# Source buckets padded to 256 rows instead of 512, four parts in a unit, adds one unit behind

## The reference

```python
Wh = h @ W + b
row, col = edge_index[0], edge_index[1]          # the edge's source, the edge's destination
sc = softplus(deg_coeff[0] * deg_v + deg_coeff[1])
dot = sum(Wh[row] * Wh[col], -1);  nr, nc = norms of Wh[row], Wh[col]
sim = dot / maximum(nr * nc, EPS)
base = adj_v * sc * (row != col)
prop_pos = segment_sum((base * relu(sim))[:, None] * Wh[col], row)
prop_neg = segment_sum((base * -relu(-sim))[:, None] * Wh[col], row)
out = scale * (coeff[0] * prop_pos + coeff[1] * prop_neg + coeff[2] * Wh)
x = layernorm(x + out)
```

## Time and profile before

| | us |
|---|---|
| median of 3 runs | 9442.85 (9428.52 to 9460.71) |
| the profiled execution | 9496.65 |
| its span, first to last instruction | 9494.9 |
| unit loop in it, first pick to last add | 8290.0 to 9446.6 |

### The profile page before, as it was taken

The page is one execution under the profiler, slowest core; times in us unless marked ns, Lnnn a source line. Parts: engine busy times, 40 slices in busy tenths (PEclk is TensorE's granted clock), DMA queues, the critical chain, the costliest instruction groups (busy, mean ns, idle before and its releaser), DMA issues. The chain is left out here.

```text
span 9494.9 us, 103424 instructions
## 1 busy us (share of the span) xinstructions
PE 5779.2 (61%) x22770; PEld 3507.7 (37%) x22771; DVE 4579.2 (48%) x10542; ACT 3305.8 (35%) x6399; POOL 5102.6 (54%) x5308
## 2 busy tenths in 40 slices
PE   0068788888840777777777524444443444499997
PEld 0034343434320333333333222222222222299997
DVE  2545555555542333333333353444444444477777
ACT  0023333333320333333333311111111111299997
POOL 5666666666656666666666555566655656500000
PEclk9978887878765777777777755555555555599998
DMA  8233333333321333333333211111111111122221
GB/s 325 80 93 111 109 107 110 109 110 106 112 62 49 98 98 103 102 103 103 106 103 104 81 30 55 52 52 53 52 51 51 53 51 53 47 59 59 60 59 52
DMA packets 566846, 800.69 MB, mean 84 GB/s; under 512 B 163210, under 2 KB 307466, under 8 KB 566506
## 3 DMA queue, kind: packets, MB, share of 16 engines
q1 hardware_dynamic: 371944, 482.15, 16.8%
q0 software_dynamic: 172640, 195.75, 9.3%
q10 hardware_dynamic: 22178, 121.99, 3.2%
HBM read 497.93 MB, written 301.41 MB: 84 GB/s over the span
## 5 line engine op out<-in xcount | busy, mean ns | idle before, releaser
L696 POOL DMA_INDIRECT rows_by_src_bucket<-arena,put_idx x1568 | 1532.8, 978 | 1019.2 <-DVE arena L1342 549.3
L625 POOL DMA_INDIRECT G<-h_rows,src_idx x1568 | 1483.2, 946 | 852.7 <-issue 456.2
L625 POOL DMA_INDIRECT G<-in_x,src_idx x1470 | 1395.7, 949 | 808.5 <-issue 432.2
L1172 DVE TENSOR_TENSOR_SCAN xd_t<-same,xd_t,ps_two 128x512 f32<-128x512 bf16 x588 | 749.1, 1274 | 1044.1 <-remote 870.0
L746 PE MATMUL ps_gv<-attr,w_attr 65*128 65x512 f32 x1568 | 1104.1, 842 | 220.4 <-issue 126.3
L749 PE MATMUL ps_gv<-arena,w_src 128*128 128x512 f32 x1568 | 1044.3, 803 | 0.0
L728 PE MATMUL ps_two<-ident,inj 128*128 128x128 f32 x2352 | 445.1, 322 | 938.1 <-DMA inj<-first_edge_rows 648.2
L928 ACT COPY arena<-ps_out 128x512 f32<-128x512 f32 x392 | 230.5, 588 | 2124.7 <-remote 1864.0
L813 PE MATMUL ps_pos<-arena 128*128 128x392 f32 x390 | 316.3, 914 | 1017.1 <-DVE arena L1195 621.9
L1234 DVE TENSOR_SCALAR arena<-ps_gv 128x512 f32<-128x512 f32 x392 | 266.5, 680 | 1228.5 <-remote 607.4
L752 PE MATMUL ps_gv<-xd_t,w_dst 128*128 128x512 f32 x1568 | 773.8, 616 | 3.5 <-issue 3.5
(11 more groups left out here) (226 smaller groups left out, 10251.1 us busy)
## 6 DMA issues: line engine op xcount, KB each, us to landing
inj<-first_edge_rows SPq DMA_DIRECT2D x588, 256.0 KB
running_sums<-arena SPq DMA_DIRECT2D x392, 256.0 KB
same<-same_dst SPq DMA_DIRECT2D x1176, 64.0 KB
rows_by_src_bucket<-zeros ACTq DMA_DIRECT2D x98, 703.5 KB
first_edge_rows<-zeros ACTq DMA_DIRECT2D x56, 896.0 KB
attr<-in_attr_t SPq DMA_DIRECT2D x392, 128.0 KB
G<-h_rows,src_idx POOLq DMA_INDIRECT x1568
rows_by_src_bucket<-arena,put_idx POOLq DMA_INDIRECT x1568
```

The lines of the kernel that those rows point to most:

```text
L625: pool.indirect_dma_start(out_, None, table_in, bass.IndirectOffsetOnAxis(ap=index, axis=0)).then_inc(s, 16)
L696: pool.indirect_dma_start(bucket_d, bass.IndirectOffsetOnAxis(ap=put_idx[:, buf, k:k + 1], axis=0), put[:, buf, k], None).then_inc(s_added ...
L1172: v.tensor_tensor_scan(xd_t[:, buf % 2], same[:, buf], ps_inj, xd_t[:, 1 - buf % 2, COLS - 1:COLS], ALU.mult, ALU.add).then_inc(s_scan, 1)
```

## The change

Buckets are padded to 256 rows (a *part*, `PART`) instead of 512, and a unit of 1024 rows holds four parts instead of two halves. With the same 200,704 edges the padding allows for 98 x 256 rows instead of 98 x 512: `UNITS` goes from 248 to 224, `UTRIPS` from 31 to 28. So each unit has four buckets: PE picks two tiles with each register, and loads eight registers in every second unit; PE's sum accumulates over two tiles, into four ranges of the bank; DVE has four adds of 64 columns instead of two, and loads four registers in every unit. DVE's add follows with a lag of one unit instead of two. The parts' bucket numbers need seven columns instead of four (`IDS`), and the table `bucket_at` lies in the first partition of the tile `attr`, which the convolutions have finished with.

```diff
-UNIT = 2 * COLS
+PARTS = 4
+PART = 2 * P
+UNIT = PARTS * PART
 NU = 8
-UNITS = -(-(EP // COLS + NT) // (2 * NU)) * NU
+UNITS = -(-(EP // PART + NT) // (PARTS * NU)) * NU
+IDS = UNITS * PARTS // P
...
-        bucket_units = bucket_d[0:BROWS].rearrange("(u a p j) f -> u p a (j f)", a=2, p=P, j=TILES)
+        bucket_units = bucket_d[0:BROWS].rearrange("(u q p j) f -> u p q (j f)", q=PARTS, p=P, j=2)
...
-        bucket_at = sb("bucket_at", [1, 2, COLS], I32)
...
+        bucket_at = attr[0:1].rearrange("p b c -> p (b c)")[:, 0:2 * UNITS * PARTS].bitcast(I32).rearrange(
+            "p (k n) -> p k n", k=2)
...
             def pick(h, buf):
-                if buf % NB == 0:
-                    pe.wait_ge(s_halves, 1)
+                if buf % 2 == 0:
+                    pe.wait_ge(s_parts, 1)
                     buckets[:] = nc.values_load_multi_w_load_instructions(
-                        bucket_at[0:1, 0, ds(h * (2 * NU) + 2 * buf, 2 * NB)], engines=(mybir.EngineType.PE,),
+                        bucket_at[0:1, 0, ds(h * (PARTS * NU) + PARTS * buf, 2 * PARTS)], engines=(mybir.EngineType.PE,),
...
             def sum_unit(h, buf):
...
+                for k in range(SLOTS):
+                    mm = pe.matmul(summed[buf % 2][:, k // 2], onehot[:, buf % NB, k], w_msg[:, buf % 2, k],
+                                   start=k % 2 == 0, stop=k % 2 == 1)
                 mm.then_inc(s_outs, 1)
...
-                for c in range(TILES):
-                    then(v.tensor_scalar(junk_, ends, half_id[:, c:c + 1], 0.0, ALU.is_le, ALU.add,
-                                         accum_out=half_bucket[:, c:c + 1]))
+                for c in range(IDS):
+                    then(v.tensor_scalar(junk_, ends, part_id[:, c:c + 1], 0.0, ALU.is_le, ALU.add,
+                                         accum_out=part_bucket[:, c:c + 1]))
...
             def add_unit(h, buf):
-                if buf % 2 == 0:
-                    dve.wait_ge(s_halves, 2)
-                    homes[:] = nc.values_load_multi_w_load_instructions(
-                        bucket_at[0:1, 1, ds(h * (2 * NU) + 2 * buf, 4)], engines=(mybir.EngineType.DVE,), min_val=0,
-                        max_val=(NT - 1) * D,
-                        skip_runtime_bounds_check_because="a count of bucket ends, at most NT - 1")[1]
+                dve.wait_ge(s_parts, 2)
+                homes = nc.values_load_multi_w_load_instructions(
+                    bucket_at[0:1, 1, ds(h * (PARTS * NU) + PARTS * buf, PARTS)], engines=(mybir.EngineType.DVE,),
+                    min_val=0, max_val=(NT - 1) * D,
+                    skip_runtime_bounds_check_because="a count of bucket ends, at most NT - 1")[1]
                 dve.wait_ge(s_outs, udone(h, buf))
-                for a in range(2):
-                    home = H[:, ds(homes[2 * (buf % 2) + a], D)]
-                    add = v.tensor_tensor(home, home, summed[buf % 2][:, a], ALU.add)
-                    if a == 0:
+                for q in range(PARTS):
+                    home = H[:, ds(homes[q], D)]
+                    add = v.tensor_tensor(home, home, summed[buf % 2][:, q], ALU.add)
+                    if q < PARTS - 1:
                         then(add)
                 add.then_inc(s_hadd, 1)
                 dve.wait_ge(s_hadd, udone(h, buf))
 
-            pipeline(dve, (weigh, 0), (add_unit, 2), steps=steps, per=8 * NU, n=NU, trips=UTRIPS)
+            pipeline(dve, (weigh, 0), (add_unit, 1), steps=steps, per=10 * NU, n=NU, trips=UTRIPS)
```

More of the change, by code:

```diff
@@ L242, in gnn @@
         onehot = tile(NB, SLOTS, P)
-        rows = [t.rearrange("p (a c) -> p a c", a=2) for t in (
+        rows = [t.rearrange("p (q c) -> p q c", q=PARTS) for t in (
             *(whole[:].rearrange("p b c -> p (b c)")[:, k * 2 * TILES * RW:(k + 1) * 2 * TILES * RW]
@@ L588, in load_unit @@
                     sp.wait_ge(s_wm, udone(h, buf, NU))
-                load(rows[buf], bucket_units[ds(h * NU + buf, 1)].rearrange("u p a c -> p (u a) c"), s_unit[buf])
+                load(rows[buf], bucket_units[ds(h * NU + buf, 1)].rearrange("u p q c -> p (u q) c"), s_unit[buf])
             pipeline(sp, (load_unit, 0), n=NU, trips=UTRIPS)
@@ L854, in pick @@
                 pe.wait_ge(s_dotted, udone(h, buf, 1))
[L855 to L858 removed]
+                for k in range(SLOTS):
+                    col = k % TILES * (D + 1)
+                    mm = pe.matmul(ps_two[:, k // TILES, col:col + D + 1], onehot_t[:, buf % 2, k],
+                                   wh_flat[:, ds(buckets[PARTS * (buf % 2) + k // 2], D + 1)], start=True, stop=True)
                 mm.then_inc(s_wr, 1)
@@ L863, in sum_unit @@
                 pe.wait_ge(s_hadd, udone(h, buf, 2))
-                for a in range(2):
-                    for j in range(TILES):
-                        mm = pe.matmul(summed[buf % 2][:, a], onehot[:, buf % NB, a * TILES + j],
-                                       w_msg[:, buf % 2, a * TILES + j], start=j == 0, stop=j == TILES - 1)
+                for k in range(SLOTS):
+                    mm = pe.matmul(summed[buf % 2][:, k // 2], onehot[:, buf % NB, k], w_msg[:, buf % 2, k],
+                                   start=k % 2 == 0, stop=k % 2 == 1)
                 mm.then_inc(s_outs, 1)
@@ L1324, in _ @@
             for k, width in enumerate((D + 1, D)):
-                v.tensor_scalar(bucket_at[0:1, k], ps_out[0:1], float(width), None, ALU.mult).then_inc(s_halves, 1)
+                for c, table in enumerate((ps_out, ps_pos)):
+                    n = min(COLS, IDS * P - c * COLS)
+                    turn = v.tensor_scalar(bucket_at[0:1, k, c * COLS:c * COLS + n], table[0:1, 0:n], float(width), None,
+                                           ALU.mult)
+                turn.then_inc(s_parts, 1)
             def place_group(i):
@@ L1359, in weigh @@
             def weigh(h, buf):
-                now = rows[buf].rearrange("p a (j f) -> p a j f", f=RW)
-                flat = rows[buf].rearrange("p a (j f) -> p (a j) f", f=RW)
+                flat = rows[buf].rearrange("p q (j f) -> p (q j) f", f=RW)
+                now = flat.rearrange("p (a j) f -> p a j f", a=2)
                 picked = ps_two[:, :, 0:TILES * (D + 1)].rearrange("p a (j f) -> p a j f", f=D + 1)
```

47 lines of the change are left out of this document (23 added, 24 removed).

## The result

| | before | after |
|---|---|---|
| median, chip A, us | 9449.92 | 9486.42 |
| ratio, 95% interval | | 1.0042 [1.0031, 1.0053] |
| median, chip B, us | 8119.79 | 8161.10 |
| ratio, 95% interval | | 1.0043 [1.0028, 1.0057] |
| profiled execution on A / its span | 9496.65 / 9494.9 | 9506.64 / 9504.9 |

The change makes the kernel slower by 0.42% as the ratio gives it; the two medians are 36.5 us apart. Chip B runs the stages ahead of the unit loop much faster, but its ratio is the same. In the two profiled executions on A those stages differ by 35 us in after's favour (the first pick is at 8255.4 instead of 8290.0), which hides most of the loop's loss in them; on the faster chips of the experiments variants of both kernels have the first pick between 6915 and 6930 us. So I read the change from the loop alone.

A forecast was written before the change was run, and what follows sets the result against it. It took PE, DVE and ACT as all near the unit loop's bound. -12 + 3 - 1 + 70 = +60 gave a span of 9555, taken over to the median as 9503 us; range 9425 to 9600.

The forecast's parts named there:

- DVE sets the pace: Unit loop: two more adds make DVE's cycle 4.97 us, above PE's 4.43; trips 40.5 us against 36.97.
- The term of -12 us: Unit loop: 28 trips of 40.5 us, 1134 us, against 1146; the saved units are nearly eaten by the adds.
- Register loads at nothing: DVE's load of four registers in every unit, 344 ns, is covered by L1382: nothing; uncovered, up to 39 us.
- The rival of 601 ns: DVE's register load takes 601 ns, first add 0.25 us later in each unit: +46, 9489 us before falls; chance 0.05.
- The lag costs nothing: Adds one unit behind: PE's sum is ready before DVE comes to its add, so no new wait costs time.
- ACT and the loads of units free: Unit loop: ACT fits in 4.62 us a unit; unit loads stay hidden, up to 1 us at the loop's start.
- The clock: Unit loop: PE's idle gaps lower its clock at every second trip's end, 14 falls of 5 us: +70 us; forecast's chance 0.63.
- PE's ordinary gap: PE idles 0.53 us ahead of its sum in every unit, between 0.37 that held the clock and 0.66 that fell.
- The clock holds: Rival: no falls in the unit loop, only DVE's pace counts: -10, 9433 us; chance 0.22.
- The adds are covered: Rival: the unit keeps its 4.62 us by PE's or ACT's pace: -111 + 2, 9334 us; chance 0.05.
- The clock stays low: Rival: PE keeps the lower clock for most of the unit loop, 1888 us against 1146: 10180 us; chance 0.05.
- The terms of +3 and -1: Setting up, with more counts, transposes, writes and two adds at the end: +3 us; smaller bucket clearing: -1 us.

The follow-up runs named there:

- One filler at the trip's end: The changed kernel with four more PE transposes in one unit of eight, the turn at the trip's end; ratio to the kernel before 0.9984.
- the kernel with two adds: The changed kernel without the adds of the third and fourth part of each unit; one execution, trips 35.71 us, unit loop 1005.6 us.
- the fillers: Extra PE transposes in the changed kernel: four in one unit of eight, ratio to the kernel before 0.9984; four in every unit, 1.0001.
- two fillers: The changed kernel with two more PE transposes in every unit; one execution, unit loop 1141.3 us.
- the kernel with split adds: The kernel before with each add of 64 columns cut into two of 32, four adds in a unit; one execution, 9666.17 us.

## Why the prediction was right

The forecast was 9503 us by a few falls of the clock; the median is 9486.42. The signs it named are there: a granted clock of 0.92 in the loop, the adds in fours, trips of two lengths. Step by step:

- **DVE sets the pace: right.** I had 4.97 us a unit and 40.5 a trip; after has 40.55. The first rows of two ordinary units stand 4.97 apart (8617.82 and 8622.80). Of the parts, the adds' step of 0.35 is (1.27 - 0.22) / 3, and a trip's end costs what the earlier trace rows gave. The term of -12 us is -10.4.
- **Register loads at nothing: right by an accident of the layout.** 344 ns at the median, as in the earlier trace rows. The rival of 601 ns did not come. But that the duration belongs to four registers at such addresses, and not to the instruction, I could not know, and did not ask.
- **The lag costs nothing: right,** and it spares some 10 us against a lag of two, which I had put at nothing once DVE is the bound. In the kernel before, where PE waits for adds, it gives 20 us even with the longer load.
- **ACT and the loads of units free: right.** DVE does not wait for the root in after, nor for a unit.
- **The clock: right in kind and place, too dear.** I had 14 falls at 5 us, 70 us; it was 14 at 4.12, 57.7 us. That the number came out exactly is luck: it was a guess between none and 27, and on chip B there were 11 long falls. The price was mis-sized for a reason: I took bounds from PE's cycle at the lower level and from the time that PE loses at the loop's start, and left out that PE's pick runs ahead of DVE by 2.0 us. The chain of the earlier trace rows is taken where PE has no lead, so it could not show this; DVE's first row against the end of the pick, in any unit, would have.
- **PE's ordinary gap.** I set 0.53, a difference of two cycles, between a 0.37 and a 0.66 that were read from the brackets of rows. In the same brackets the ordinary gap of after is about 0.37, as wide as the widest of before. What is new is how many there are: by the waits, 154 of 0.43 on average with the wider ones at the trips' ends, where there were 88 of 0.26.
- **Which gap.** I took both the ordinary gap and the trip's end for possible causes. One filler at the trip's end keeps the clock up, so it is the end. I had priced it as one gap of 1.1 us. In the rows it is split: the pick starts 1.06 behind the turn instead of 0.89, and the sum 8597.28 - 8594.68 = 2.60 behind the pick, where without a gap it is 1.73 (8705.29 to 8707.02 in the kernel with two adds). That is 0.17 + 0.87 = 1.04, the size I had, in two pieces.
- **Not explained: why about every second end.** 14 of 27 ends bring a fall. These are the rows at an end without a fall. They are the same as at the end with one, to 0.02 us:

```profile
8551.24 1.99 PE L872 MATMUL ps_out<-arena 128*128 128x64 f32 x16 [0.44 <-DVE arena L1392]
...
8554.12 2.00 PE L864 MATMUL ps_two<-arena 128*128 x16
8556.73 1.99 PE L872 MATMUL ps_pos<-arena 128*128 128x64 f32 x16 [0.61 <-DVE arena L1392]
```

What tells them apart is not in PE's rows at the end, and no run here was made to find it. One thing that DVE's rows show is a slip. In four successive falls, each two trips behind the last, DVE's first long wait gets shorter by 0.1 and the second longer: 2.02 and 2.48, 1.92 and 2.57, 1.83 and 2.66, 1.73 and 2.76. Then the very next trip has a fall, with 2.03 and 2.47 again. So the falls keep a rhythm that is not quite the trips' own, and whether an end brings one may depend on where in that rhythm it comes; this is not shown. "TensorE: Matmul & The Clock Gate" of the Trainium skill, section "A second HAM failure mode: psum-queue depth-cycling", says that frequent short idle spells make the clock swing. This case agrees in part: the fall shown above follows a gap of 0.61 at a trip's end, but 13 of 27 such ends bring none, and 0.37 in every unit does not lower the clock.

- **The rivals.** *The clock holds* did not come true for after, but its time can be seen: with the fillers the ratio is 0.9984 and 1.0001, and the 10 us less that I had forecast for it lie between. *The adds are covered* did not come true either, and became true in part when the adds were placed elsewhere; I had asked whether they are hidden, not what would hide them. (In *The clock stays low* the sum 9442.85 + 742 gives 10185, not 10180; nothing rests on it.)
- **The total.** The loop is +45.3 us where my terms for it were -12 + 70 = +58: the falls' term is 70 - 57.7 = 12.3 less, DVE's pace gave back 1.6 less than I had, and the loop's start and end, for which I had nothing, gave 2.0. The terms of +3 and -1 lie ahead of the loop or behind it, where the two profiled executions differ by 35 us anyway, so no run here shows them. The median is +36.5, with an interval of 29 to 50 (0.31% to 0.53%), which holds the loop's 45.

## What to carry to other kernels

Once an engine other than PE sets the pace, PE's gaps can cost more than the pace itself, as here (57.7 us against a gain of 10.4). Look for the step of the loop whose gap is widest, here its end, and try a few instructions of cheap PE work there. Price a fall of the clock by PE's loss less its lead over the engine that waits for it. Small dependent instructions of DVE, like the adds of 32 and 64 columns here, are priced by their number more than their width, and can be hidden in each other's shadow: then a change that saves units by adding such instructions pays.

## What the runs showed of the hardware that I had not expected

- **A register load's time depends on how many words it reads and from where.** Four words from a word number that is a multiple of four: 344 ns at the median in each of the kernels that do so. Two words: 528. Four words from two words further: about 970. Only the difference between 344 and these costs DVE time. The Trainium skill ("DMA: Bandwidth & Descriptors", section "Latency and other measured facts") gives about 600 ns as a floor; the measurement stays below it for the first two.
- **Falls of the clock come in different lengths.** 13.6 us is the usual one in after, 3.4 us the one with two fillers. A short one costs nothing there, and 1.2 us in the kernel with split adds, where PE has 0.48 us of lead instead of 1.7.
- **More work can be faster.** 0.44 us of useless transposes in a trip of 40 us take 55 us off the changed kernel.
- **Chips differ ahead of the loop, not in it.** The kernel before takes 8120 us on one and 9521 on another; in after the first pick is at 6926 and 8255, while a trip without a fall lasts 40.60 and 40.55.
